# The experts' phase written out tile by tile, its value products shared between GpSimd and VectorE, attention blocks added in pairs, and weights loaded on condition

## The chip, the cores and the metric

The kernel runs on one core of one Trainium2 chip. The metric is the device time of one execution in microseconds; the time before is the median of three runs. The profile is of one further execution.

## The reference

All is float32. With x of [4, 2048, 256] the result is `x + attention(xn) + ffn(xn)`, where xn is x after a layer norm without gains.

`attention` works on each token alone, across its 16 heads of 16:

```python
Q, K, V = (xn @ Wq + bq), (xn @ Wk + bk), (xn @ Wv + bv)   # [b, s, 16, 16]
Q, K = rope(Q), rope(K)                    # one token's q and k turn by the same angles
score = einsum('bsid,bsjd->bsij', Q, K) / 4
out = einsum('bsij,bsjd->bsid', softmax(score), V)
```

`ffn` is a mixture block in two steps. The first, called `_mla`, projects queries, keys and values, computes a causal attention per head along 2048 positions and adds its output projection. The second, called `_moe`, takes the normed result row by row:

```python
logits = t @ gate_w                       # 8 experts
top_v, top_i = top_k(logits, 2)
gates = softmax(top_v)
hid = silu(t @ w1[e])                     # 256 -> 512
y   = hid @ w2[e]                         # 512 -> 256
out = sum over the row's two experts of gate * y
```

In the kernel, `attention` is done in blocks of 128 tokens, whose q, k and v stand in `head_qkv`: for each token 16 x 16 scores, their softmax and the product with v. Half of the 64 blocks are done earlier in the program, on GpSimd beside other work; the experts' phase does the other 32.

## The kernel before

The program has five phases: projections, attention along the positions, output projection and routing, experts, and the final store. The routing phase writes each token's row twice, once for each of its two experts, into `sorted_rows` (the profile's `rows_by_expert`), sorted by expert. It also makes `table_i`: for each of 71 tiles of 256 rows (`N_TILE`) the expert and the first row. Its first column is, for tile n, the number of experts whose tiles end at or before n (L1571 to L1580), so it never falls from one tile to the next. `acc` in DRAM collects the result.

`phase4_experts` does two things at once, on all engines.

The experts' part goes tile by tile. SP loads the tile's rows (`load_tile`, L1781, one of four buffers, `RB`; it waits until the add of tile n - 4 has landed, `y_added`), and the expert's two weight matrices, 512 KB each, into one of two buffers (L1784 and L1786; it waits until tile n - 2 is multiplied, `y_done`). PE transposes the rows (L1978), multiplies by w1 (L1990) and w2 (L2003); its order for a tile is `hidden(n)`, `transpose_rows(n + 1)`, `second(n)`. ScalarE applies SiLU (L1949), copies the transposed rows (L1923) and scales the result by the gate into `y` (L1966). GpSimd adds the tile into `acc` with two indirect scatters (`add_tile`, L1822). Before it issues them it waits until the add before has landed, that of the tile and that of the block, because both read and write rows of `acc`.

The blocks' part goes one block to two tiles. SP loads q, k and v of a block (`load_block`, L1772). ScalarE copies q to PSUM (L1929). VectorE multiplies q by k (L1870, 4096 elements a partition), sums over the head's 16 (L1873), takes the maximum (L1875) and subtracts it (L1879). ScalarE takes the exponential (L1936). VectorE sums the rows (L1884) and inverts (L1886). GpSimd multiplies the probabilities by v (`weigh_values`, L1806) in three pieces: 8 heads in the even tile, 4 and 4 in the odd one, with the block's own add (L1829, 128 KB from SBUF into 128 rows of `acc`) between the last two. VectorE sums these products (L1893) and multiplies by the inverse (L1896).

The order on each engine's queue is the order in which the code is written; nothing is scheduled at run time. The groups of four tiles (`quads`) run as a loop from the third group on, and so does VectorE's body. All waits are written by hand. Many are `wait_apart`, a wait with a second instruction that increments an unused semaphore.

## Time and profile before

| | |
|---|---|
| median of 3 runs | 3068.91 us (3065.43 to 3079.44) |
| the profiled execution, its own time | 3062.26 us |
| its span | 3060.5 us |
| PE busy | 2571.4 us, 84% |
| VectorE (DVE) busy | 2334.0 us, 76% |
| ScalarE (ACT) busy | 1572.3 us, 51% |
| GpSimd (POOL) busy | 2328.0 us, 76% |
| moved by DMA | 404.89 MB, mean 132 GB/s |
| weight transfers | 142 of 512 KB, each in one loop of two a tile |

The shares are means over the whole span; what bounds one phase is read from that phase. A row of the profile names the line of the kernel, the engine, the operation and the tiles, and the idle time before it with what ended it.

### The profile page before, as it was taken

The numbers are of one execution on the slowest core, as the hardware profiler recorded it, in microseconds if no ns is written. First come the engines' busy times: TensorE is split into PE (matmuls) and PEld (weight loads), VectorE is DVE, ScalarE is ACT, GpSimd is POOL, SyncE is SP. The second block draws the span as 40 slices with busy tenths as digits, with TensorE's granted clock in tenths as the row PEclk, the third lists the DMA queues.
The fourth block names the chain that finished last, engine by engine and source line by source line (L and its number), as shares of the span: only waits on it lengthen the run. The fifth ranks groups of instructions, "written<-read, shape, count | busy, mean of one in ns | idle before, by whom it ended". The sixth has DMA issues, their size and how long they took to land. (4 is left out here: it accounts for less than half of the span.)

```text
span 3060.5 us, 59749 instructions
## 1 busy us (share of the span) xinstructions
PE 2571.4 (84%) x21356; PEld 1316.2 (43%) x21356; DVE 2334.0 (76%) x3621; ACT 1572.3 (51%) x2325; POOL 2328.0 (76%) x1230
## 2 busy tenths in 40 slices
PE   7998978999999999999999999766757768777782
PEld 4544432333333333333333333255646656666662
DVE  4567858999999999998999984045639888988860
ACT  2322236777777767777677777622323333333330
POOL 5443359788988889888988889746748888888882
PEclk9999999999999999999999999877778989889886
DMA  5886541323332223332233311387566667666766
GB/s 195 273 269 203 180 149 52 85 51 86 82 88 77 64 84 82 90 79 64 82 83 85 75 40 42 97 259 252 171 186 171 164 167 167 170 163 164 173 160 165
DMA packets 296054, 404.89 MB, mean 132 GB/s; under 512 B 32040, under 2 KB 221832, under 8 KB 295560
## 3 DMA queue, kind: packets, MB, share of 16 engines
q1 hardware_dynamic: 264360, 357.80, 39.1%
q0 software_dynamic: 31200, 39.73, 7.6%
q10 hardware_dynamic: 256, 4.19, 0.4%
q8 instruction: 148, 2.42, 0.3%
q14 instruction: 90, 0.74, 0.1%
HBM read 251.16 MB, written 158.23 MB: 134 GB/s over the span
## 5 line engine op out<-in xcount | busy, mean ns | idle before, releaser
L1044 DVE TENSOR_REDUCE p_piece_max<-p_ring 128x1 f32<-128x512 f32 (+3 forms) x2160 | 1293.7, 654 | 137.4 <-PE p_ring L157 67.7
L1102 ACT ACTIVATE p_probs<-p_st 128x1024 f32<-128x1024 f32 (+3 forms) x1280 | 1079.0, 897 | 413.8 <-PE p_st L1165 216.6
L1165 PE MATMUL p_st<-unit_q,unit_k 64*128 64x512 bf16 (+3 forms) x3520 | 434.6, 349 | 42.1 <-ACT p_probs L1102 25.4
L1183 PE MATMUL p_pv<-p_probs,unit_vg 128*32 128x512 f32 (+3 forms) x3520 | 412.0, 542 | 0.0
L1806 POOL TENSOR_TENSOR p_pv<-p_pr,p_qkv 128x1024 f32<-128x1024 f32 (+1 forms) x96 | 403.1, 4206 | 1.4 <-ACT p_pr L1936 1.4
L982 POOL TENSOR_TENSOR p_terms<-p_head_p,p_head_in 128x4096 f32<-128x4096 f32 x32 | 348.5, 10890 | 0.1
L1822 POOL DMA_INDIRECT acc<-p_y,p_rows x142 | 224.8, 1583 | 105.2 <-issue 42.0
L2003 PE MATMUL p_y_ps<-p_w,p_hid 128*128 128x256 f32 x1136 | 300.4, 425 | 3.4 <-ACT p_hid L1949 3.3
L170 PE MATMUL p_ring<-unit_k,unit_q 64*128 64x512 bf16 (+3 forms) x1600 | 271.7, 353 | 27.9 <-DVE p_piece_max L1044 25.4
L961 POOL TENSOR_TENSOR p_terms<-p_head_in 128x4096 f32<-128x4096 f32 x32 | 283.4, 8856 | 8.2 <-POOL p_head_s L969 4.4
L1990 PE MATMUL p_hid_ps<-p_rT,p_w 128*128 128x256 f32 x1136 | 259.8, 382 | 7.1 <-issue 4.3
L988 POOL TENSOR_TENSOR p_terms<-p_terms 128x2048 f32<-128x2048 f32 (+2 forms) x96 | 252.4, 2630 | 17.1 <-POOL p_terms L988 11.4
L966 POOL TENSOR_TENSOR p_terms<-p_terms 128x2048 f32<-128x2048 f32 (+2 forms) x96 | 252.0, 2625 | 17.1 <-POOL p_terms L966 11.4
L2003 PEld LDWEIGHTS p_y_ps<-p_w,p_hid 128*128 128x128 f32 x1136 | 242.3, 219 | 43.9 <-issue 2.8
L1990 PEld LDWEIGHTS p_hid_ps<-p_rT,p_w 128*128 128x128 f32 x1136 | 216.4, 191 | 40.2 <-issue 10.7
L1165 PEld LDWEIGHTS p_st<-unit_q,unit_k 64*128 64x128 bf16 x3520 | 136.6, 95 | 219.9 <-ACT p_probs L1102 130.9
L170 PEld LDWEIGHTS p_ring<-unit_k,unit_q 64*128 64x128 bf16 x1600 | 71.4, 93 | 363.8 <-DVE p_piece_max L1044 351.1
L1978 PE MATMUL p_rT_ps<-ident,p_rows 128*128 128x128 f32 x284 | 54.6, 325 | 191.8 <-DMA p_rows<-rows_by_expert 191.8
L1893 DVE TENSOR_REDUCE p_oh<-p_pv 128x256 f32<-128x4096 f32 x32 | 141.4, 4420 | 96.1 <-POOL p_pv L1806 95.2
L1165 PE MATMUL p_st<-p_q,p_k 34*128 34x512 bf16 (+7 forms) x1600 | 194.3, 346 | 8.1 <-ACT p_probs L1102 6.7
L1183 PE MATMUL p_pv<-p_probs,p_vg 128*32 128x512 f32 (+3 forms) x1600 | 186.3, 540 | 0.0
L1445 POOL DMA_INDIRECT rows_by_expert<-p_th,p_pos x128 | 132.4, 1034 | 37.6 <-issue 34.8
(184 smaller groups left out, 3610.0 us busy)
## 6 DMA issues: line engine op xcount, KB each, us to landing
p_w<-ffn_w SPq DMA_DIRECT2D x142, 512.0 KB, 5.6
qk_parts<-p_parts SPq DMA_DIRECT2D x64, 384.0 KB, 3.4
head_qkv<-p_heads SPq DMA_DIRECT2D x16, 1536.0 KB, 6.5
p_rows<-rows_by_expert SPq DMA_DIRECT2D x71, 258.0 KB, 3.7
unit_q<-qk_parts SPq DMA_DIRECT2D x132, 128.0 KB, 3.2
unit_k<-qk_parts SPq DMA_DIRECT2D x132, 128.0 KB, 3.6
v_padded<-p_vx SPq DMA_DIRECT2D x16, 1024.0 KB, 8.2
p_head_in<-head_qkv SPq DMA_DIRECT2D x32, 384.0 KB, 4.0
```

Of the source, the lines that this page charges most:

```text
L170: last[half] = nc.tensor.matmul(banks[half][:, k * width:(k + 1) * width], q6[rows, h + k, i * P:(i + 1) * P], k6[rows, h + k, pc * CT:pc ...
L961: step(nc.gpsimd.tensor_tensor(terms[:, :, :, :], head_in[:, u, 0, :, :].unsqueeze(2).to_broadcast([P, H, H, DH]), head_in[:, u, 1, :, :]. ...
L966: step(nc.gpsimd.tensor_tensor(terms[:, :, :, 0:width], terms[:, :, :, 0:width], terms[:, :, :, width:2 * width], ALU.add), before + 2 + k)
L982: step(nc.gpsimd.tensor_tensor(terms[:, :, :, :], head_p[:, u, :, :].unsqueeze(2).to_broadcast([P, H, DH, H]), head_in[:, u, 2, :, :].rear ...
L988: step(nc.gpsimd.tensor_tensor(terms[:, :, :, 0:width], terms[:, :, :, 0:width], terms[:, :, :, width:2 * width], ALU.add), before + 2 + k)
L1044: nc.vector.tensor_reduce(piece_max[:, n % 2, h:h + heads, i, pc], ring_ps[g % RING][:, 0:heads * width].rearrange("p (h k) -> p h k", h=h ...
L1102: nc.scalar.activation(probs[:, 2 * turn_of(s, i) + u, :, 0:width], st_ps[u][:, :, 0:width], ACT.Exp).then_inc(probs_done, 1)
L1165: last = nc.tensor.matmul(st_ps[u][:, half, 0:width], k6[s][rows, PAIR * second + u, kt * P:(kt + 1) * P], q6[s][rows, PAIR * second + u, ...
L1183: last = nc.tensor.matmul(pv_ps[hh * VW:(hh + 1) * VW, skip:CT], vg[s][:, kt, hh * VW:(hh + 1) * VW], probs[:, 2 * turn_of(s, i) + hh % PA ...
L1806: ins = nc.gpsimd.tensor_tensor(pv[:, u, h, :, :], pr[:, u, h, :].unsqueeze(2).to_broadcast([P, count, DH, H]), qkv[:, u, 2, :].rearrange( ...
L1990: last = nc.tensor.matmul(hid_ps[i][:, f * ROW_TILE:(f + 1) * ROW_TILE], w1[:, u, k, (2 * i + f) * P:(2 * i + f + 1) * P], rT[:, k, :], st ...
L2003: last = nc.tensor.matmul(y_ps[t][:, 0:D], hid[:, f, t * P:(t + 1) * P], w2[:, u, f, :], start=f == 0, stop=f == FB - 1)
```

## The change

It touches `phase4_experts` alone.

- The loops over groups of four tiles are gone: each engine's code is written out for all 71 tiles and 32 blocks, with waits on constants and without the second instruction of `wait_apart`. Where a block's steps come among the tiles is in tables (`STARTS`, `WEIGHED`, `ADDED`, `STORED`, `LOADED`, `COPIED`, `SHIFTED`). With `SPAN` 64 and 32 blocks `STARTS[m]` is 2m, so a block still begins every two tiles.
- Of the 16 heads GpSimd multiplies ten (`HP`), five in each of two tiles. VectorE multiplies the other six in `weigh_tail`. ScalarE writes their probabilities to PSUM and the ten's to SBUF, with two exponentials.
- VectorE's sum of the products goes to PSUM (`o_ps`) instead of SBUF, and the multiplication by the inverse reads it there.
- Finished blocks are stored by SP into `attn_rows` in DRAM, and GpSimd adds two neighbouring blocks at once, 256 KB from DRAM, in the 16 tiles 10, 14, ..., 70; the tile's second piece of products is cut into three and two heads around it.
- q, k and v have three buffers (`QB`) instead of two. The first three blocks are loaded at tile 0, later ones a tile or two earlier than before.
- The two weight loads of a tile carry a condition: they are done only where the tile's expert is another than that of tile n - 2, whose weights lie in the same buffer.

The diff, cut to its core:

```diff
+
+    STARTS = [m * SPAN // NB for m in range(NB + 4)]
+    PIECES = {2: (5, 5), 3: (4, 3, 3)}
...
+    WEIGHED = {n: (m, heads, heads.stop == HP) for m in range(NB) for n, heads in pieces(m)}
+    ADDED = {STARTS[2 * k + 4] + 2: k for k in range(NB // 2)}
+    STORED = {STARTS[m + 2] + 3: m for m in range(NB)}
+    LOADED = {max(0, STARTS[m] - 1): m for m in range(QB, NB)}
+    COPIED = {STARTS[m]: m for m in range(NB)}
+    SHIFTED = {STARTS[m + 1]: m for m in range(NB)}
...
+            def load_block(m):
+                if m >= QB:
+                    sp.wait_ge(pv_done, m - QB + 1)
+                    sp.wait_ge(tail_done, m - QB + 1)
+                sp.dma_start(qkv[:, m % QB, :, :].rearrange("p i d -> p (i d)"), head_qkv[block_of(m, 1)]
+                             ).then_inc(qkv_loaded[m % QB], 16)
+
+            def store_block(m):
+                sp.wait_ge(oh_done, m + 1)
+                sp.dma_start(attn_rows[block_of(m, 1)], oh[:, m % 2, :, :].rearrange("p i d -> p (i d)")
+                             ).then_inc(oh_stored[m % 2], 16)
+
+            experts = []
+            for n in range(N_TILE):
+                u = n % 2
+                e = sp.value_load(table_i[0:1, 0, n:n + 1], min_val=0, max_val=E - 1)
+                row = sp.value_load(table_i[0:1, 1, n:n + 1], min_val=0, max_val=SORTED - ROW_TILE)
+                if n >= RB:
+                    sp.wait_ge(y_added, 16 * RT * (n - RB + 1))
+                sp.dma_start(rows[:, n % RB, :, :], sorted_rows[bass.ds(row, ROW_TILE), :].rearrange("(t p) d -> p t d", p=P)
+                             ).then_inc(rows_loaded[n % RB], 16)
+                if n >= 2:
+                    sp.wait_ge(y_done, n - 1)
+                changed = None if n < 2 else e != experts[n - 2]
+                sp.dma_start(w1[:, u, :, :], w["ffn_w1"][bass.ds(e, 1), :, :].rearrange("a (k p) f -> p (a k) f", p=P),
+                             cond=changed).then_inc(w_loaded[u], 16)
+                sp.dma_start(w2[:, u, :, :], w["ffn_w2"][bass.ds(e, 1), :, :].rearrange("a (k p) f -> p (a k) f", p=P),
+                             cond=changed).then_inc(w_loaded[u], 16)
+                experts.append(e)
+                if n == 0:
+                    for m in range(QB):
+                        load_block(m)
+                if n in LOADED:
+                    load_block(LOADED[n])
+                if n in STORED:
+                    store_block(STORED[n])
...
+            def weigh(m, heads, last):
+                pool.wait_ge(exp_done, m + 1)
+                if m >= 2:
+                    pool.wait_ge(o_done, m - 1)
+                u, count = m % 2, heads.stop - heads.start
...
+            pairs = [0]
+
+            def add_tile(n):
+                pool.wait_ge(y_copied, n + 1)
+                if n:
+                    pool.wait_ge(y_added, 16 * RT * n)
+                if pairs[0]:
+                    pool.wait_ge(pair_added, 16 * pairs[0])
...
+            def add_pair(k, tiles):
+                for u in range(2):
+                    pool.wait_ge(oh_stored[u], 16 * (k + 1))
+                pool.wait_ge(y_added, 16 * RT * tiles)
+                n = block_of(2 * k, 1)
+                rows_of_pair = lambda a: a.rearrange("(r s) d -> r (s d)", s=8)
+                nc.gpsimd.dma_start(rows_of_pair(acc[n * P:(n + 2) * P, :]),
+                                    rows_of_pair(attn_rows[n:n + 2, :, :].rearrange("a p d -> (a p) d")),
+                                    accum_op=ALU.add, max_dma_last_dim=4 * 8 * D).then_inc(pair_added, 16)
+                pairs[0] += 1
+
+            for n in range(N_TILE):
+                if n:
+                    add_tile(n - 1)
+                weighed = WEIGHED.get(n)
+                if n not in ADDED:
+                    if weighed:
+                        weigh(*weighed)
+                    continue
+                if weighed:
+                    m, heads, last = weighed
+                    weigh(m, slice(heads.start, heads.stop - 2), False)
+                add_pair(ADDED[n], n)
+                if weighed:
+                    weigh(m, slice(heads.stop - 2, heads.stop), last)
+            add_tile(N_TILE - 1)
+            pool.wait_ge(y_added, 16 * RT * N_TILE)
+            pool.wait_ge(pair_added, 16 * NB // 2)
...
+            def weigh_tail(m):
+
+                u, count = m % 2, H - HP
+                dve.wait_ge(exp_done, m + 1)
+                nc.vector.tensor_reduce(psum[:, 0:HP], pr[:, u, :, :], AX_X, ALU.add)
+                nc.vector.tensor_reduce(psum[:, HP:], s_ps[u][:, HP:, :], AX_X, ALU.add).then_inc(psum_done, 1)
+                nc.vector.tensor_tensor(
+                    pv[:, u, HP:, :, :],
+                    s_ps[u][:, HP:, :].unsqueeze(2).to_broadcast([P, count, DH, H]),
+                    qkv[:, m % QB, 2, :].rearrange("p (j d) -> p d j", d=DH).unsqueeze(1).to_broadcast([P, count, DH, H]),
+                    ALU.mult).then_inc(tail_done, 1)
+                dve.wait_ge(psum_done, m + 1)
                 nc.vector.reciprocal(inv[:, u, :], psum[:, :]).then_inc(inv_done, 1)
...
+            def finish(m):
+                u = m % 2
+                dve.wait_ge(pv_done, m + 1)
+                dve.wait_ge(tail_done, m + 1)
+                nc.vector.tensor_reduce(o_ps[:, u * D:(u + 1) * D].rearrange("p (i d) -> p i d", d=DH), pv[:, u, :, :, :],
+                                        AX_X, ALU.add).then_inc(o_done, 1)
+                dve.wait_ge(o_done, m + 1)
+                dve.wait_ge(inv_done, m + 1)
+                if m >= 2:
+                    dve.wait_ge(oh_stored[u], 16 * (m // 2))
+                nc.vector.tensor_tensor(oh[:, u, :, :], o_ps[:, u * D:(u + 1) * D].rearrange("p (i d) -> p i d", d=DH),
                                         inv[:, u, :].unsqueeze(2).to_broadcast([P, H, DH]), ALU.mult).then_inc(oh_done, 1)
...
+            for m in range(NB + 2):
+                if m >= 2:
+                    finish(m - 2)
+                if 0 < m <= NB:
+                    weigh_tail(m - 1)
+                if m < NB:
+                    score(m)
...
+            def probabilities(m):
+                u = m % 2
+                act.wait_ge(sm_done, m + 1)
+                if m >= 2:
+                    act.wait_ge(inv_done, m - 1)
+                    act.wait_ge(pv_done, m - 1)
+                nc.scalar.activation(pr[:, u, :, :], sm[:, 0:HP, :], ACT.Exp)
+                nc.scalar.activation(s_ps[u][:, HP:, :], sm[:, HP:, :], ACT.Exp).then_inc(exp_done, 1)
```

## Rows read from the trace of the kernel before

**Rows 1.** The page's first line: the span.

```profile
span 3060.5 us, 59749 instructions
```

**Rows 2.** Windows, 2300 to 2957 us: window, length, busy time (instructions), clock, DMA, GB/s.

```profile
2300.00:2957.00 657.00, 497.42 (x2160) 420.33 (x2159) 575.60 (x239) 248.24 (x419) 548.22 (x238) 0.89 0.69 167
```

**Rows 3.** Groups by form, same window: busy us, mean ns | idle before, releasers.

```profile
L1806 POOL TENSOR_TENSOR p_pv<-p_pr,p_qkv 128x1024 f32<-128x1024 f32 x60 | 197.4, 3291 | 0.0
L1822 POOL DMA_INDIRECT acc<-p_y,p_rows x118 | 187.1, 1586 | 49.1 <-issue 37.9 <-DMA acc<-p_y,p_rows 7.5 <-DMA acc<-p_oh 3.7
...
L1806 POOL TENSOR_TENSOR p_pv<-p_pr,p_qkv 128x2048 f32<-128x2048 f32 x30 | 181.3, 6045 | 0.0
L1896 DVE TENSOR_TENSOR p_oh<-p_oh,p_inv 128x256 f32<-128x256 f32 x30 | 145.9, 4863 | 2.3
...
L1893 DVE TENSOR_REDUCE p_oh<-p_pv 128x256 f32<-128x4096 f32 x29 | 128.2, 4420 | 72.0 <-POOL p_pv L1806 71.1 <-DMA acc<-p_oh 0.6 <-issue 0.3
...
L1829 POOL DMA_DIRECT2D acc<-p_oh x30 | 27.7, 923 | 59.6 <-DMA acc<-p_y,p_rows 54.1 <-ACT p_pr L1936 3.9 <-issue 1.5
...
L1879 DVE TENSOR_TENSOR p_sm<-p_q_ps,p_smax 128x256 f32<-128x256 f32 x30 | 12.7, 424 | 1.0
...
L1884 DVE TENSOR_REDUCE p_psum<-p_pr 128x16 f32<-128x256 f32 x30 | 12.2, 406 | 0.0
...
L1886 DVE RECIPROCAL p_inv<-p_psum 128x16 f32<-128x16 f32 x30 | 7.6, 253 | 1.0
```

**Rows 4.** Lines L1896 and L1870 by themselves: duration min/median/max, first and last start.

```profile
L1896 DVE TENSOR_TENSOR p_oh<-p_oh,p_inv x32: 424/4746/5844, 2297.5 to 2983.4; 128x256 f32<-128x256 f32 x32
...
L1870 DVE TENSOR_TENSOR p_prod<-p_q_ps,p_qkv x30: 4359/4361/4364, 2302.9 to 2944.3; 128x4096 f32<-128x4096 f32 x30
```

**Rows 5.** The chain that ended last: start us, us, what.

```profile
2646.82 6.85 DMA acc<-p_y,p_rows
...
2656.45 6.12 DMA acc<-p_y,p_rows
...
2982.80 3.70 DMA acc<-p_y,p_rows
...
2989.23 6.05 DMA acc<-p_y,p_rows
```

**Rows 6.** DMA issues, median us to landing; then landing times of L1829, of L1822.

```profile
p_w<-ffn_w SPq DMA_DIRECT2D x122, 512.0 KB, 5.7
p_rows<-rows_by_expert SPq DMA_DIRECT2D x61, 258.0 KB, 3.7
...
DMA to landing us min/median/max: 2.8/3.1/5.4
...
DMA to landing us min/median/max: 3.7/5.1/7.7
```

**Rows 7.** Timeline, VectorE near 2288, GpSimd near 2970 and 3022 us.

```profile
2287.84 0.42 DVE L1879 TENSOR_TENSOR p_sm<-p_q_ps,p_smax 128x256 f32<-128x256 f32 x1
...
2970.54 1.55 POOL L1822 DMA_INDIRECT acc<-p_y,p_rows  x1 [0.30 <-issue]
2971.55 3.37 POOL L1806 TENSOR_TENSOR p_pv<-p_pr,p_qkv 128x1024 f32<-128x1024 f32 x1
2974.94 0.93 POOL L1829 DMA_DIRECT2D acc<-p_oh  x1
...
3022.59 1.56 POOL L1822 DMA_INDIRECT acc<-p_y,p_rows  x1 [0.30 <-issue]
```

**Rows 8.** Timeline of SP's queue, two stretches.

```profile
2643.67 0.35 SPq L1772 DMA_DIRECT2D p_qkv<-head_qkv  x1
...
2646.81 0.42 SPq L1786 DMA_DIRECT2D p_w<-ffn_w  x1
...
2975.67 0.98 SPq L1786 DMA_DIRECT2D p_w<-ffn_w  x1
...
2987.35 0.37 SPq L1784 DMA_DIRECT2D p_w<-ffn_w  x1
```

More of the change, by code:

```diff
@@ L1691, in phase4_experts, with pieces @@
     sorted_rows, acc, table_i = SHARED["sorted"], SHARED["acc"], SHARED["table"]
-    QUADS, ALL_QUADS = NB // 2, (N_TILE + 3) // 4
-    IN_LAST = N_TILE - 4 * (ALL_QUADS - 1)
     RT = ROW_TILE // P
     FB = F // P
-    RB = 4
+    RB, QB = 4, 3
+    HP = 10
+    SPAN = 64
+    STARTS = [m * SPAN // NB for m in range(NB + 4)]
+    PIECES = {2: (5, 5), 3: (4, 3, 3)}
+    def pieces(m):
+        tiles = range(STARTS[m + 1], STARTS[m + 2])
+        counts = PIECES[len(tiles)]
+        return [(n, slice(sum(counts[:k]), sum(counts[:k + 1]))) for k, n in enumerate(tiles)]
+    WEIGHED = {n: (m, heads, heads.stop == HP) for m in range(NB) for n, heads in pieces(m)}
[4 more added lines that the diff above has]
+    SHIFTED = {STARTS[m + 1]: m for m in range(NB)}
+    assert all(ADDED[n] * 2 + 1 in [m for at, m in STORED.items() if at < n] for n in ADDED)
+    assert max(ADDED) < N_TILE and max(STORED) < N_TILE and len(ADDED) == NB // 2 and len(LOADED) == NB - QB
     with ExitStack() as ctx:
@@ L1732, in phase4_experts @@
         y_added = sem("p4_y_added")
-        qkv_loaded = [sem(f"p4_qkv_loaded{i}") for i in range(2)]
+        qkv_loaded = [sem(f"p4_qkv_loaded{i}") for i in range(QB)]
         q_copied = sem("p4_q_copied")
@@ new lines, in _ @@
+            copy_rows(0)
+            for n in range(N_TILE):
+                for k in range(2):
+                    act.wait_ge(hid_done, 2 * n + k + 1)
+                    if n:
+                        act.wait_ge(y_done, n)
+                    nc.scalar.activation(hid[:, 2 * k:2 * k + 2, :].rearrange("p k t -> p (k t)"), hid_ps[k][:, :],
+                                         ACT.Silu).then_inc(silu_done, 1)
+                if n + 1 < N_TILE:
+                    copy_rows(n + 1)
+                if n in SHIFTED:
+                    probabilities(SHIFTED[n])
+                if n in COPIED:
+                    copy_q(COPIED[n])
+                act.wait_ge(y_done, n + 1)
+                if n >= RB:
+                    act.wait_ge(y_added, 16 * RT * (n - RB + 1))
+                for t in range(RT):
+                    last_copy = nc.scalar.activation(y[:, n % RB, t, :], y_ps[t][:, 0:D], ACT.Copy,
+                                                     scale=rows[:, n % RB, t, D:D + 1])
+                last_copy.then_inc(y_copied, 1)
@@ L1993, in hidden, with second @@
                     last.then_inc(hid_done, 1)
-            def second(n, u):
-                pe.wait_ge(y_copied, n)
+            def second(n):
+                if n:
+                    pe.wait_ge(y_copied, n)
                 for k in range(2):
-                    pe.wait_ge(silu_done, 2 + 2 * n + k + 1)
+                    pe.wait_ge(silu_done, 2 * n + k + 1)
                     for t in range(RT):
                         for f in range(k * FB // 2, (k + 1) * FB // 2):
-                            last = nc.tensor.matmul(y_ps[t][:, 0:D], hid[:, f, t * P:(t + 1) * P], w2[:, u, f, :],
+                            last = nc.tensor.matmul(y_ps[t][:, 0:D], hid[:, f, t * P:(t + 1) * P], w2[:, n % 2, f, :],
                                                     start=f == 0, stop=f == FB - 1)
                 last.then_inc(y_done, 1)
-            transpose_rows(0, 0, 1)
-            def body(g):
-                for i in range(tiles_of(g)):
-                    n, u = 4 * g + i, i % 2
-                    hidden(n, u, 2 * g + i // 2)
-                    if not (static(n) and n == N_TILE - 1):
-                        transpose_rows(n + 1, (i + 1) % RB, g + 1 + (i + 1) // RB)
-                    second(n, u)
-            quads(pe, body)
+            transpose_rows(0)
+            for n in range(N_TILE):
+                hidden(n)
+                if n + 1 < N_TILE:
+                    transpose_rows(n + 1)
+                second(n)
 def phase5_combine(nc, apart, res_v, attn_v, pos_v, gates_v, expert_rows, out_v):
```

208 lines of the change are left out of this document (38 added, 170 removed).

## The prediction

> **What bounds the kernel now.** I read the page first, for the span [rows 1]. Shares of the whole span decide nothing here, since the change touches only the experts' phase (lines 1685 to 2017), so I cut that stage out. Its block 1 is scored at 2287.84 us and its last scatter is issued at 3022.59 us [rows 7]. In the even middle of it PE is busy 76%, VectorE 88%, GpSimd 83% and the DMA engines 69% [rows 2]. Again nobody is full, so something is waited for in turn. VectorE's product (L1870) starts at 2302.9 for the first and at 2944.3 for the last of 30 blocks [rows 4]: 641.4 / 29 = 22.1 us a block, which is two tiles, 11.06 us a tile.
>
> The chain that ended last says what those 22.1 us are [rows 5]. It is the adds into acc, one after the other: a tile's second scatter starts at 2646.82 and takes 6.85 us to land, the next tile's starts at 2656.45 and takes 6.12, then the block's own add. The step from a landing to the next tile's second scatter is 2656.45 - 2646.82 - 6.85 = 2.8 us (1.9 from one scatter to the next, as their 1.59 and 0.3 of issue make it, so some 0.9 from a landing until GpSimd starts again). So: 2.8 + 6.5 for a tile, the same for the next, and for the block's add 3.1 in the median [rows 6] with 0.9 to pick it up: 22.6, against 22.1 measured. GpSimd's products lie in the shadows of these landings: its waits for landings sum to only 54.1 + 7.5 + 3.7 us [rows 3], so it is the second bound, close behind. VectorE waits 72 us for GpSimd's products before L1893. PE waits for rows that are loaded late, a consequence.
>
> Two facts decide the rest. First, why a landing takes 6.5 us. The one from 2982.80 takes 3.70; the last weight load before it was issued at 2975.67, seven us earlier. The one from 2989.23 takes 6.05, with a weight load issued at 2987.35 and the next one right behind [rows 5, 8]. While GpSimd multiplies it can be short too: the scatter at 2970.54 had landed when the block's add, which waits for it, began at 2974.94, so in under 4.4 us, though a product ran from 2971.55 [rows 7]. So it is the weights in flight, not GpSimd's work. Second, L1896, 256 elements, takes 4746 ns in the median and 424 at least [rows 4]. L1879 has as many elements and takes 424 in the mean [rows 3]; it has one operand in PSUM, L1896 both in SBUF, and L1896's longest, 5844, stays just under GpSimd's product of 6045. It is held while GpSimd multiplies, not slow.
>
> **The change, part by part.**
> - Weights. The table of experts does not fall along the tiles (L1571 to L1580 count the experts that lie behind), so there are at most 7 changes, and each reloads at most both buffers: 2 + 14 = 16 tiles load instead of 71, 32 transfers instead of 142. That takes 110 / 71 x 0.5 MB, some 0.8 MB, of each tile's traffic away. The landing should fall to 3.7 to 4.4 us on most tiles; I take 4.0. The rest of the traffic (rows, 258 KB in 3.7 us [rows 6]) stays beside it.
> - GpSimd's products. Ten heads instead of 16, in two pieces of five. From 1024 elements in 3.29 and 2048 in 6.05 us [rows 3], 2.69 ns an element: 1280 take 3.98. A tile's two scatters take 2 x 1.59 + 0.3, less 0.56 where the product's row overlaps: 2.9. With 0.17 of hand-over a plain tile is 7.05 us of GpSimd. The landing chain of the same tile is 2.8 + 4.0 = 6.8. These are level, so GpSimd sets it.
> - The pair's add: 16 of 256 KB from DRAM instead of 32 of 128 KB from SBUF, each in one tile of four. The trace has no such transfer. Bounds: 2.8 us below (fastest block's add) and 7.7 above (the slowest landing of any scatter) [rows 6]; I take 4.5, nearer to the block's add, since its bytes double and its issue is the same instruction. That tile: 1.9 + 4.0 + 0.9 until the pair is issued (three heads, 2.6 us, lie inside), then 4.5 + 0.9 until the next scatter (two heads inside): 12.2. Four tiles: 3 x 7.05 + 12.2 = 33.3, or 16.7 a block.
> - VectorE. Removed: L1896's hold, 4.86 down to 0.42, because its input moves to PSUM. Added: the product of six heads, 1536 elements; L1870 gives 4096 in 4.36 and L1879 256 in 0.42, so 1.03 ns an element and 1.74 us; the row sums in two parts, 0.31 + 0.24 instead of 0.41. A block is 4.36 + 4.42 (L1873, a sum of 4096 like L1893's) + 0.42 (the maximum, of 256 like L1884's 0.41) + 0.42 (scores), 4.42 + 0.42 (finish), 1.74 + 0.55 + 0.25 (tail): 17.0, and with some 0.03 in each of ten joints 17.3 us [rows 3, 4]. That is above GpSimd's 16.7, so **VectorE becomes the bound**.
> - Does anything feed VectorE late? After its maximum is subtracted (time s), ScalarE's exponential is done at s + 1.0; GpSimd has the two pieces by s + 12 in a plain round and s + 16.3 in one with a pair. VectorE wants them at s + 17.3. The slack is 1 us in each second round, used up when the pair's landing reaches 5.5. ScalarE waits for s in order, with the y copies behind it and PE's second product behind those. Until it is back at that place it has at most its own work of a block and half of PE's before it. Its own is 248.2 us over 29.7 blocks, 8.4; PE's is 2160 matmuls at 36 a tile, so 60 tiles in 497.4, 8.3 each at a mean clock of 0.89, 7.4 at full clock, 14.8 a block [rows 2]. 8.4 + 7.4 = 15.8 is inside 17.3, and so is PE by itself.
> - SP. load_block still waits for GpSimd, but three blocks deep and one block earlier; the rows behind it come at s + 17.5 to 21.5, wanted by 21.4. store_block waits for work finished by then. I count nothing for it; VectorE covers it, and without that cover it is some 1 us in each second round. The second instruction of each wait goes away and the loops are written out, also under VectorE's cover, where at most the 0.6 us a tile that stands as "issue" before scatters (37.9 us over 59 tiles [rows 3]) could be gained without it.
>
> Some of these near misses will cost; I add 0.4 to the floor of 17.3 and take **17.7 us a block**.
>
> **The sum.** Block 1 is scored at 2287.84 now [rows 7], by the pace of the tiles, and block 2 can't come before; with the tail product it is 2291. Block 31: 2291 + 30 x 17.7 = 2822. Then seven tiles remain: block 31's products until s + 12, pair 14 until s + 25, four tiles at 2.8 + 3.7 = 6.5, pair 15, the last scatter: s + 58.5. Last scatter at 2880.5; behind it the same 3060.5 - 3022.59 = 37.9: span 2918.4, 142 us less than 3060.5. The execution's own time lies 1.8 above its span, 3062.3, and the median of the runs 6.6 above that: 3068.9 - 142 = **2927**.
>
> **A rule weighed.** The row: the block's add, 128 KB, lands in 3.1 us in the median [rows 6]. The Trainium skill (DMA: Bandwidth & Descriptors, Anatomy of one DMA) fits a GpSimd-issued transfer as 2.0 us plus the bytes at 436 GB/s, 2.3 us for this one. The trace here is 0.8 above. By the rule the pair would land in 2.6 and GpSimd's four tiles be 31.4; the sum, set by VectorE, would be the same.
>
> **The rivals.**
> - *The feeding is late.* Pair landing of 7.7, or the shared order of ScalarE and SP, makes GpSimd 36.5 a four, 18.3, and the joints cost another 0.7: 19.0 a block, 2966. For it: 1 us of slack. Against: the weights loading beside the scatters, which made the longest landings, are mostly gone. 0.22.
> - *The landing stays at 6.5*, because rows and GpSimd's own traffic suffice, or because the condition does not skip. Then a tile is 9.2, the pair's 14.6: 42.2 a four, 21.1 a block; 2291 + 633, about 100 more than my case: 3029. Against: 3.70 at 2982.80 [rows 5]. 0.08.
> - *The tail product is held like L1896.* GpSimd starts its product at the same exponential, 4.0 long: 21.3 a block, 3035. Against: L1870, one operand in PSUM, takes 4359 to 4364 in all 30 with GpSimd busy 83% [rows 2, 4]. The Trainium skill (SBUF — State Buffer, SBUF: two separate sides) has VectorE and GpSimd exclude each other only for two SBUF inputs or a two-port mode; by that the tail is free, at 17.3. 0.04.
> - *Slower: conditional transfers are dear on SP.* Its queue needs now some 3.6 us from one block load (2643.67) through the rows' load to the end of the tile's second weight load (2646.81 + 0.42) [rows 8]. It decides above 11.2 us a tile (22.4 a block brings back the old time), so (11.2 - 3.6) / 2 = 3.8 for each of two transfers. If a skipped one held the queue as long as a real one takes to land, 5.7 [rows 6], a tile is 15.0 and a block 30.0: 30 x 12.3 = 369 more than my case, 3296. The lower end is a skip that costs no more than an issue now, 0.42, and that is hidden. No row shows a condition; I lean to the low end, since nothing in a skip has to wait for data. 0.04.
>
> **Chances and range.** My case 0.62 (2895 to 2950 alone). Faster by over 0.5% 0.94, same 0.02, slower 0.04; the before runs spread 0.46%, so about 0.5% is what can be told. Below: no waits at all, 17.0 a block (-21), and a tail at PE's pace (-10), 2896. Above: 19.9 a block, +66, 2993. Range 2895 to 2990 leaves out the last three rivals, 0.16.
>
> **What the profile would show.** L1896's successor at 0.42; the tail product at 1.7; VectorE at 95% or more of the middle stage, with its wait for GpSimd near nothing; scatters that land in 4 us; 32 weight transfers at the most; PE's clock near full, since its pauses for rows shrink. I am wrong if landings stay above 5.5, if the pair's takes over 6, or if VectorE waits above 1 us a block.

## The result and the profile after

| | before | after |
|---|---|---|
| median of 4 runs | 3071.62 us (3065.43 to 3079.44) | 2926.18 us (2925.28 to 2926.78) |
| ratio | | 0.9519, 95% interval 0.9500 to 0.9538 |
| span of the profiled execution | 3060.5 us | 2923.9 us |

The kernel is 145 us faster. The predicted 2927 us and the measured time agree within 1 us, but not all terms do. First the page of the kernel after: the span, the busy times, and SP's DMA queue.

```profile
span 2923.9 us, 58265 instructions
...
PE 2546.4 (87%) x21356; PEld 1302.0 (45%) x21356; DVE 2283.6 (78%) x3685; ACT 1570.9 (54%) x2357; POOL 2180.7 (75%) x1196
...
q1 hardware_dynamic: 224968, 304.32, 35.1%
```

The same row of the kernel before:

```profile
q1 hardware_dynamic: 264360, 357.80, 39.1%
```

SP's queue moved 357.80 MB before. It now carries 4.19 MB of block stores more, so 357.80 + 4.19 - 304.32 = 57.7 MB are gone: at 0.524 MB each, 110 transfers. 32 of 142 were done: SP's queue shows them in tiles 0, 1, 8, 9, 16, 17, 25, 26, 34, 35, 41, 42, 50, 51, 58 and 59, two each.

The window in the middle of the experts' phase, as in [rows 2]:

```profile
2300.00:2800.00 500.00, 444.36 (x2046) 382.15 (x2044) 495.15 (x282) 236.69 (x430) 390.57 (x196) 0.95 0.60 126
```

VectorE was 88% busy and is 99%. GpSimd fell from 83 to 78%. PE's granted clock rose from 0.89 to 0.95, while its wait for rows before the transposes fell from 154.8 us in 657 to 41.9 in 480; that the one made the other is not shown.

Groups by form, 2320 to 2800 us of the kernel after, against [rows 3]:

```profile
L1835 POOL DMA_INDIRECT acc<-p_y,p_rows x108 | 170.1, 1575 | 77.2 <-issue 36.1 <-DMA acc<-attn_rows 24.9 <-ACT p_y L1963 14.8
L1818 POOL TENSOR_TENSOR p_pv<-p_pr,p_qkv 128x1280 f32<-128x1280 f32 x42 | 169.7, 4041 | 4.6 <-ACT p_q_ps L1943 4.6
...
L1905 DVE TENSOR_REDUCE p_o_ps<-p_pv 128x256 f32<-128x4096 f32 x28 | 123.7, 4418 | 1.0 <-POOL p_pv L1818 1.0
...
L1893 DVE TENSOR_TENSOR p_pv<-p_q_ps,p_qkv 128x1536 f32<-128x1536 f32 x27 | 74.4, 2757 | 0.0
...
L1845 POOL DMA_DIRECT2D acc<-attn_rows x13 | 11.5, 884 | 7.4 <-DMA acc<-p_y,p_rows 5.2 <-DVE p_o_ps L1905 1.6 <-issue 0.5
```

VectorE's sum L1905 (L1893 before) waited 71.1 us for GpSimd's products in 657 us; now it waits 1.0 in 480. GpSimd has idle time instead, most of it before its scatters: 24.9 us for the pair's add to land and 14.8 for `y`. The tail product, L1893 now, takes 2757 ns where I had 1740.

Lines by themselves: duration min/median/max in ns, first and last start; then landing times of the tiles' scatters (L1835) and of the pairs' adds (L1845).

```profile
L1911 DVE TENSOR_TENSOR p_oh<-p_o_ps,p_inv x32: 423/424/427, 2304.6 to 2848.2; 128x256 f32<-128x256 f32 x32
...
DMA to landing us min/median/max: 3.6/4.0/7.5
...
DMA to landing us min/median/max: 4.0/4.6/5.5
```

L1911 is L1896's successor: 4746 ns in the median before [rows 4], 424 each time now. One block of VectorE in the timeline (start us, us):

```profile
2600.67 0.42 DVE L1884 TENSOR_TENSOR p_sm<-p_q_ps,p_smax 128x256 f32<-128x256 f32 x1
2601.01 4.42 DVE L1905 TENSOR_REDUCE p_o_ps<-p_pv 128x256 f32<-128x4096 f32 x1
2605.46 0.42 DVE L1911 TENSOR_TENSOR p_oh<-p_o_ps,p_inv 128x256 f32<-128x256 f32 x1
2605.80 0.31 DVE L1891 TENSOR_REDUCE p_psum<-p_pr 128x10 f32<-128x160 f32 x1
2606.03 0.25 DVE L1892 TENSOR_REDUCE p_psum<-p_q_ps 128x6 f32<-128x96 f32 x1
2606.20 2.76 DVE L1893 TENSOR_TENSOR p_pv<-p_q_ps,p_qkv 128x1536 f32<-128x1536 f32 x1
2608.88 0.24 DVE L1899 RECIPROCAL p_inv<-p_psum 128x16 f32<-128x16 f32 x1
2609.04 4.35 DVE L1875 TENSOR_TENSOR p_prod<-p_q_ps,p_qkv 128x4096 f32<-128x4096 f32 x1
2613.43 4.43 DVE L1878 TENSOR_REDUCE p_q_ps<-p_prod 128x256 f32<-128x4096 f32 x1
2617.89 0.42 DVE L1880 TENSOR_REDUCE p_smax<-p_q_ps 128x16 f32<-128x256 f32 x1
2618.35 0.42 DVE L1884 TENSOR_TENSOR p_sm<-p_q_ps,p_smax 128x256 f32<-128x256 f32 x1
```

From one L1884 to the next is 17.68 us, with no idle stretch. The ten durations sum to 18.02: where a row does not need the one before, it starts 0.08 us before that one's end (2601.01 against 2600.67 + 0.42), so the joints give time back.

SP's queue nearby: a tile's two weight loads skipped, the next tile's rows load, and the first of that tile's weight loads, done.

```profile
2602.05 0.09 SPq L1798 DMA_DIRECT2D p_w<-ffn_w  x1
2602.24 0.08 SPq L1800 DMA_DIRECT2D p_w<-ffn_w  x1
2604.22 0.39 SPq L1793 DMA_DIRECT2D p_rows<-rows_by_expert  x1
2609.74 0.39 SPq L1798 DMA_DIRECT2D p_w<-ffn_w  x1
```

A skipped one holds the queue for 0.08 to 0.09 us here, a done one for 0.39.

Where the 136.6 us of span came from, by the starts of the subtraction: from block 1 to block 31 it took 2953.65 - 2287.84 = 665.8 us and takes 2831.38 - 2299.79 = 531.6, 134.2 less. The tiles after block 31 take 56.3 instead of 68.9 (12.6 less) and what follows 36.2 instead of 37.9 (1.7 less). Against this block 1 starts 12.0 us later, of which 9.8 lie ahead of the phase: its first weight load is issued at 2255.5 us instead of 2245.7.

### The profile page after: what moved, and what is told of

It is laid out like the page before. It is cut to its first block and busy times, and to the rows that moved or that the text cites. A ratio compares the mean times of both kernels' runs of the same rounds, so it can differ in the third digit from the quotient of the medians.

```text
span 2923.9 us, 58265 instructions
## 1 busy us (share of the span) xinstructions
PE 2546.4 (87%) x21356; PEld 1302.0 (45%) x21356; DVE 2283.6 (78%) x3685; ACT 1570.9 (54%) x2357; POOL 2180.7 (75%) x1196
## 3 DMA queue, kind: packets, MB, share of 16 engines
q1 hardware_dynamic: 224968, 304.32, 35.1%
q10 hardware_dynamic: 256, 4.19, 0.4%
## 5 line engine op out<-in xcount | busy, mean ns | idle before, releaser
L1165 PE MATMUL p_st<-unit_q,unit_k 64*128 64x512 bf16 (+3 forms) x3520 | 433.1, 348 | 41.6 <-ACT p_probs L1102 24.9
L1835 POOL DMA_INDIRECT acc<-p_y,p_rows x142 | 223.4, 1573 | 135.8 <-ACT p_y L1963 49.5
L2000 PE MATMUL p_y_ps<-p_w,p_hid 128*128 128x256 f32 x1136 | 278.9, 402 | 11.1 <-ACT p_hid L1951 10.8
L1818 POOL TENSOR_TENSOR p_pv<-p_pr,p_qkv 128x1280 f32<-128x1280 f32 (+2 forms) x78 | 259.6, 3328 | 26.8 <-ACT p_q_ps L1943 26.8
L2000 PEld LDWEIGHTS p_y_ps<-p_w,p_hid 128*128 128x128 f32 x1136 | 226.0, 204 | 45.2 <-issue 13.2
L1875 DVE TENSOR_TENSOR p_prod<-p_q_ps,p_qkv 128x4096 f32<-128x4096 f32 x32 | 139.6, 4364 | 30.0 <-ACT p_q_ps L1934 30.0
L1905 DVE TENSOR_REDUCE p_o_ps<-p_pv 128x256 f32<-128x4096 f32 x32 | 141.4, 4418 | 4.9 <-POOL p_pv L1818 4.9
```

The costliest lines, as they stand in the source:

```text
L1165: last = nc.tensor.matmul(st_ps[u][:, half, 0:width], k6[s][rows, PAIR * second + u, kt * P:(kt + 1) * P], q6[s][rows, PAIR * second + u, ...
L1818: ins = nc.gpsimd.tensor_tensor(pv[:, u, heads, :, :], pr[:, u, heads, :].unsqueeze(2).to_broadcast([P, count, DH, H]), qkv[:, m % QB, 2, ...
L2000: last = nc.tensor.matmul(y_ps[t][:, 0:D], hid[:, f, t * P:(t + 1) * P], w2[:, n % 2, f, :], start=f == 0, stop=f == FB - 1)
```

## The experiments

All kernels below compute the whole reference. "Period" is the mean distance of the blocks' subtractions, from block 1 to block 31, in the profiled execution: 22.19 us before, 17.72 after. A round is the time from one block's subtraction to the next one's; a plain round has no pair's add on GpSimd. Kernels that ran beside one another are compared by medians, others also by their ratio to the kernel before.

### Each part undone

**All weights loaded.** In the kernel after:

```diff
-                changed = None if n < 2 else e != experts[n - 2]
+                changed = None
```

> The changed kernel with the condition taken off the weight loads: both are done for each of the 71 tiles. My theory: weights in flight lengthen the landings of the scatters (4.5 us in the median with the condition, 5.1 before), the chain of adds becomes the bound again, 42.2 us for four tiles or 21.1 a block instead of 17.7: 30 x 3.4 = 102 us more, about 3028. Rival, the gain is VectorE's and GpSimd's shorter work alone and the landings stay hidden behind products: 17.7 a block, 2926, within 0.5%. A middle result of 18.5 to 20 a block (2950 to 2995) would say that the landings lengthen, but less than the earlier chain had it.

Measured: 2976.28 us (2961.18 to 3003.86), ratio 0.9648 (0.9607 to 0.9688). That is 40 (by ratios) to 50 us (by medians) given back, half of what I expected. (The 4.5 us in the expectation is a slip: with the condition the scatters land in 4.0.) The profiled execution was its slowest: its span is 78 us above that of the kernel after. Its group of VectorE's sum, 2320 to 2800 us, and the landings of L1835 and L1845:

```profile
L1905 DVE TENSOR_REDUCE p_o_ps<-p_pv 128x256 f32<-128x4096 f32 x25 | 110.5, 4422 | 45.2 <-POOL p_pv L1818 45.1
...
DMA to landing us min/median/max: 3.6/4.9/8.4
...
DMA to landing us min/median/max: 4.1/6.1/7.6
```

The landings rise by 0.9 and 1.5 us with the weights in flight, and the wait for GpSimd is back. But rounds without a pair's add still take 17.7 to 17.9 us; those with one, but for the first, take 18.5 to 26.6. So a plain round has cover for a longer landing, and only the pair's tile lets it through.

Why less than the 102 us: the first six rounds stay at 17.7. Beyond that, the chain waits for the second scatter of a tile, the last to land in all 71, and how long that one takes depends on when the weights come. In the kernel before, 53 of the 71 second scatters had a weight load issued between 0.5 us ahead of them and 2 us behind, as here (a piece of the chain, then SP's queue):

```profile
2613.20 6.21 DMA acc<-p_y,p_rows
...
2613.80 0.37 SPq L1784 DMA_DIRECT2D p_w<-ffn_w  x1
```

These 53 landed in 6.7 us in the median, and the six with no weight load near them (none from 6 us ahead until they landed) in 3.8. In the new order with all weights 32 of 71 meet a load in that way and land in 6.7 too; over all 71 the median is 5.1, where it was 6.4 in the kernel before. I had carried the 6.5 of the old order into the new one. How much of the shortfall this makes, and why the runs spread from 2961 to 3004 us, is not shown.

**Value sum back in SBUF.** L1905 sums into `oh`, L1911 reads it there:

```diff
-                nc.vector.tensor_reduce(o_ps[:, u * D:(u + 1) * D]..., pv[:, u, :, :, :],
+                nc.vector.tensor_reduce(oh[:, u, :, :], pv[:, u, :, :, :],
...
-                nc.vector.tensor_tensor(oh[:, u, :, :], o_ps[:, u * D:(u + 1) * D]...,
+                nc.vector.tensor_tensor(oh[:, u, :, :], oh[:, u, :, :],
```

The wait for the earlier store of `oh` moves ahead of the sum with it.

> The changed kernel with the sum of the value products back in SBUF, so that the multiplication by the inverse has both operands in SBUF. My theory: it is held while GpSimd multiplies; GpSimd's piece now lies differently, from about s + 1.9 to s + 5.9 where VectorE wants to multiply at s + 4.8, so a hold of 0 to 1.5 us in a plain round and up to 3 in others: the row L1911 has a least value of 424 ns and a mean of 1.2 to 2.5 us, a block takes 18.4 to 19.8, the time is 2947 to 2990. Rival: the hold in the kernel before was a waiting for something else, and the row stays at 424: 2926.

Measured: 2936.43 us (2935.57 to 2940.65), ratio 0.9537 (0.9505 to 0.9569), period 18.18. The multiplication by itself:

```profile
L1910 DVE TENSOR_TENSOR p_oh<-p_oh,p_inv x32: 424/1038/2449, 2303.1 to 2860.0; 128x256 f32<-128x256 f32 x32
```

It is held again, up to 2449 ns, but takes 1.0 us in the median and not 4.7, and 0.9 in the mean, where I expected 1.2 to 2.5. The block and the time also stay below what I expected. GpSimd's product lies differently beside it in this order of work. With two SBUF inputs it is held, with one in PSUM it never was (427 at most). The Trainium skill (SBUF — State Buffer, SBUF: two separate sides) has just this condition, and both traces agree. The move to PSUM is worth 10 us by the medians and 5 by the ratios in this order of work, not the 4.3 us a block that the old order would suggest.

**Blocks added one by one**, each in its own tile, still from DRAM:

```diff
-    ADDED = {STARTS[2 * k + 4] + 2: k for k in range(NB // 2)}
+    ADDED = {STARTS[m + 4]: m for m in range(NB)}
```

> The changed kernel with each block added alone, 128 KB from DRAM, in every second tile, instead of two at once in every fourth. My theory: GpSimd's four tiles hold two waits for landings instead of one: 2 x 7.05 + 2 x (1.9 + 4.0 + 0.9 + 3.7 + 0.9 = 11.4) = 36.9, 18.5 a block against VectorE's 17.7, so 20 to 30 us more, about 2950. Rival, VectorE covers it since GpSimd has slack in plain rounds: same time, 2926.

Measured: 2973.66 us (2970.22 to 2979.08), ratio 0.9655 (0.9621 to 0.9689), period 18.93: 42 to 48 us given back, about twice what I expected. Its sum L1904, the adds' group with their waits, 2320 to 2800 us, and their landing:

```profile
L1904 DVE TENSOR_REDUCE p_o_ps<-p_pv 128x256 f32<-128x4096 f32 x26 | 115.1, 4425 | 30.7 <-POOL p_pv L1818 30.7
...
L1844 POOL DMA_DIRECT2D acc<-attn_rows x24 | 20.8, 868 | 42.2 <-DMA acc<-p_y,p_rows 42.2
...
DMA to landing us min/median/max: 3.3/3.6/4.3
```

Two blocks cost 2 x 3.6 of landing apart and 4.6 together, but what weighs as much is the wait before each add: 42.2 us for the scatter ahead of it, against 5.2 with pairs.

**All 16 heads on GpSimd**, in two pieces of eight:

```diff
-    HP = 10
+    HP = 16
...
-    PIECES = {2: (5, 5), 3: (4, 3, 3)}
+    PIECES = {2: (8, 8), 3: (6, 5, 5)}
```

> The changed kernel with all 16 heads' value products on GpSimd, eight in each of two tiles, none on VectorE. My theory: GpSimd takes 6.05 + 2.9 + 0.17 = 9.1 us in a plain tile and 13.1 in one with a pair, 40.5 for four, 20.2 a block, and VectorE's 15 lie inside: 30 x 2.5 = 76 us more, about 3002. Rival, the products lie in the shadow of the landings as they did before (chain of a tile 2.8 + 4.0 = 6.8, under 9.1 only if landings stay short), and the share given to VectorE brought nothing: 2926.

Measured: 3004.97 us (3003.21 to 3010.86), ratio 0.9755 (0.9724 to 0.9787), period 19.96, for the most part rounds of 18.3 and 21.8 in turn. In 2320 to 2800 us VectorE's sum, L1897, waits as the row says:

```profile
L1897 DVE TENSOR_REDUCE p_o_ps<-p_pv 128x256 f32<-128x4096 f32 x24 | 106.3, 4428 | 117.1 <-POOL p_pv L1817 117.1
```

So the sharing is the dearest single part, 73 to 79 us, and GpSimd bounds without it, as reckoned.

### Parts done alone on the kernel before

**The condition only**, in `load_tile`:

```diff
+                changed = e != sp.value_load(table_i[0:1, 0, bass.ds(n - 2, 1)], min_val=0, max_val=E - 1)
...
-                             ).then_inc(w1_loaded[u], 16)
+                             cond=changed).then_inc(w1_loaded[u], 16)
```

> The kernel before with one part of the change alone: the condition on the weight loads (with one more register load a tile on SP). My theory: its chain of landings shortens. The even tile is then set by GpSimd's own 9.1 us, the odd tile by 1.9 + 4.3 + 0.9 for the scatter and 3.1 + 0.9 for the block's add, 11.1: 20.2 a block instead of 22.1, 60 us less, a ratio of 0.98. Rival 1, weights in flight do not matter by themselves: ratio 1.00. Rival 2, all of the landing's surplus was the weights' and the products are hidden entirely: 18.0 a block, a ratio of 0.96.

Measured: 3006.10 us (3002.97 to 3007.78), ratio 0.9750 (0.9734 to 0.9766), period 20.19 where 20.2 was expected. The multiplication that was L1896, then the landings of the scatters and of the blocks' adds:

```profile
L1899 DVE TENSOR_TENSOR p_oh<-p_oh,p_inv x32: 424/4754/5340, 2308.0 to 2928.5; 128x256 f32<-128x256 f32 x32
...
DMA to landing us min/median/max: 3.6/3.9/8.1
...
DMA to landing us min/median/max: 3.0/3.1/4.0
```

This is the cleanest evidence for the first step: nothing but the weights changed (and one register load a tile), the scatters' landing went from 5.1 [rows 6] to 3.9, that of the second scatters alone from 6.4 to 3.9, and GpSimd's wait for landings before a block's add from 54.1 us in 657 to 5.2 in 480. The two profiled executions lie 59 us apart, as expected, the medians 77. What is left is the held multiplication, still 4754 ns: VectorE is 96% busy, with 4.3 us a block of it hold, and GpSimd 93%.

**Written out only**: the loops and second instructions gone and three buffers for q, k and v, with every other part undone (all weights, 16 heads on GpSimd, the sum in SBUF, single adds from SBUF in the old tiles).

```diff
-    ADDED = {STARTS[2 * k + 4] + 2: k for k in range(NB // 2)}
+    ADDED = {STARTS[m + 2] + 1: m for m in range(NB)}
```

> All parts of the change undone except the writing out (and three buffers for q, k and v): all weights loaded, 16 heads on GpSimd in 8, 4 and 4, the sum in SBUF, each block added alone from SBUF after the odd tile's scatters. My theory: the loops and the second instruction of each wait lay beside the chain of landings; at most 0.6 us a tile of issue, mostly hidden: a ratio of 0.990 to 1.00. Rival: writing out by itself brings 2% or more, by earlier loads and no loop ends, 0.98 or less.

Measured: 3098.30 us (3092.19 to 3104.38), ratio 1.0077 (1.0048 to 1.0106), period 23.08. Written out alone brings nothing and costs 0.8% (0.5 to 1.1), a little above the range that I expected. The landing of its scatters is 5.3 us in the median and that of the second ones 6.8 (6.4 before), with the chain of adds as the bound as before: two a block make some 0.7 of the 0.9 us. Why they land later was not isolated.

### What the tail product costs, and what is behind it

**Values turned for VectorE.** L1893 reads v with a step of 16 elements. ScalarE writes a copy in the order that VectorE reads (0.64 us), and only VectorE uses it:

```diff
+                nc.scalar.copy(vt[:, m % 2, :, :], qkv[:, m % QB, 2, :].rearrange("p (j d) -> p d j", d=DH)).then_inc(vt_copied, 1)
...
-                    qkv[:, m % QB, 2, :].rearrange("p (j d) -> p d j", d=DH).unsqueeze(1).to_broadcast([P, count, DH, H]),
+                    vt[:, u, :, :].unsqueeze(1).to_broadcast([P, count, DH, H]),
```

> The changed kernel where ScalarE copies the block's values, turned so that the 16 that are multiplied together lie side by side, and VectorE's tail product reads this copy. One more wait and one copy of 256 elements a block on ScalarE, GpSimd as before. My theory: the tail product takes 2.76 us instead of 1.74 because it reads its values with a step of 16 elements, so it falls to some 1.7 us, a block to 16.7, and with GpSimd's own 16.7 to 17 behind it the time falls by 20 to 30 us, about 2900. Rival: it is the operand in PSUM with a short repeat, or GpSimd at work on the same tiles; then the row stays at 2.76 and the time at 2926.

Measured: 2923.32 us (2915.94 to 2926.27), ratio 0.9473 (0.9453 to 0.9494), period 17.59. VectorE's sum in 2320 to 2800 us, and the tail product, L1896 here:

```profile
L1908 DVE TENSOR_REDUCE p_o_ps<-p_pv 128x256 f32<-128x4096 f32 x28 | 123.8, 4423 | 26.5 <-POOL p_pv L1820 26.5
...
L1896 DVE TENSOR_TENSOR p_pv<-p_q_ps,p_vt 128x1536 f32<-128x1536 f32 x28 | 48.9, 1747 | 0.0
```

The product falls from 2757 to 1747 ns, so the step was the whole of my error in it. The time hardly moves by the medians (3 us) and by the profiled spans (2923.9 and 2922.9). By the ratios it is 14 us, but the kernel before varied by 12 us from one series to the next and the kernel after by 1, so I go by the medians. Plain rounds take 16.67 us and are 1.0 shorter. Rounds with a pair take 17.0 to 18.2 and 19.8 to 21.0 in turn from block 11 on, since VectorE now waits 26.5 us for GpSimd, and GpSimd for its own adds:

```profile
L1837 POOL DMA_INDIRECT acc<-p_y,p_rows x108 | 170.1, 1575 | 82.4 <-issue 42.0 <-DMA acc<-attn_rows 33.6 <-ACT p_y L1969 6.6
```

The long ones come behind the tiles that still load weights. From one pair's add to the next, GpSimd's four tiles take 33.3 to 35.3 us where no weights are loaded meanwhile, and 34.8 to 38.7, four of five above 36, where those of two tiles are; VectorE's floor for them is 33.3. Scatters issued near these loads land in 5.4 us in the median, all others in 3.9. That the weights cause the delay is shown by the condition alone above; here it is the timing that speaks for it. GpSimd's floor is right behind VectorE's.

**Eleven heads on GpSimd**, to test that from the other side (`HP = 11`, pieces of six and five; v as in the kernel after):

> The changed kernel with 11 heads on GpSimd (six and five) and five on VectorE. My theory, VectorE is the bound and GpSimd has slack: VectorE's block loses 0.46 and is 17.2, GpSimd's four tiles gain 2 x 0.69 and are 34.7, 17.3 a block: 10 to 14 us less, about 2914. Rival, GpSimd and its landings are level with VectorE already: 18.0 a block or more, 2930 to 2945.

Measured: 2932.82 us (2929.89 to 2933.89), ratio 0.9509 (0.9493 to 0.9524), period 17.73. The time is in the rival's range, but the period is neither the 17.3 of my theory nor the rival's 18.0: plain rounds take 17.24 us as expected, but from block 13 on most rounds with a pair take 18.35 and more, so that the mean is that of the kernel after. What VectorE gains GpSimd takes back.

**Values turned and nine heads** (`HP = 9`, pieces of five and four):

> The kernel of values_turned with nine heads on GpSimd (five and four) and seven on VectorE. If the turned copy makes a head cost VectorE 0.27 us instead of 0.46, VectorE's block is 16.9 and GpSimd's 16.2: VectorE alone is the bound, about 2903, equal to or 5 us above values_turned. If values_turned is held by GpSimd's 16.7 to 17.2, this is the faster one, down to 2895. If turning brings nothing, a block is 18.1 and the time 2940.

Measured: 2913.99 us (2909.56 to 2917.60), ratio 0.9450 (0.9431 to 0.9468), period 17.20, plain rounds 16.93. This is 9 us less than with ten heads and turned values, run beside it, though VectorE's plain round is 0.26 longer: GpSimd did hold that kernel. It does not reach 2903, since late rounds are left, of 18.4 to 19.1 us, the first at block 17. The tail product of seven heads takes 2015 ns, so a turned head costs VectorE the 0.27 us that I took.

**Values turned, uneven pieces.** Ten heads, but eight and two in the rounds with a pair's add. The add lies in the first of the round's two tiles, within the block's first piece of five heads (not the second), which it cuts into three and two. Here that piece has eight heads, cut into four and four:

```diff
-        counts = PIECES[len(tiles)]
+        counts = (8, 2) if m % 2 == 0 and m >= 4 else PIECES[len(tiles)]
...
-                    weigh(m, slice(heads.stop - 2, heads.stop), last)
+                    weigh(m, slice(heads.stop - 4, heads.stop), last)
```

> The kernel of values_turned (ten heads on GpSimd), where in the rounds with a pair's add GpSimd multiplies eight heads in the pair's tile, four before and four after its issue, and only two in the next tile. Theory: the surplus of values_turned over VectorE's 16.67 (17.59 in the mean, in the rounds with a pair) is GpSimd's lateness; the two waits for landings in the pair's tile, 4.3 and 4.9 us, hold four heads each for nothing, so GpSimd gains 2 us in each such round and VectorE's 16.7 holds in nearly all: 27 us less than values_turned, a ratio of 0.940 to 0.943. Rival: the joints are SP's and ScalarE's order, and the pieces' place changes nothing: 0.947.

Measured: 2912.28 us (2911.46 to 2914.34), ratio 0.9471 (0.9444 to 0.9498), period 17.24. That is 11 us below the even pieces by the medians of two series, and nothing by the ratios, which give just the rival's 0.947. The periods (17.59 and 17.24) and the profiled spans (2922.9 and 2910.5) side with the medians, but the two never ran beside one another, so the gain of the pieces alone is not settled, and it is less than half of the 27 us that I expected. The kernel after, again beside it:

> The changed kernel as it is, beside the others on one chip, to have their differences without that of the chips. Ratio 0.950 to 0.954, a block 17.7, no theory differs.

Measured: 2924.97 us (2924.71 to 2932.29), ratio 0.9518 (0.9489 to 0.9546). Turning and uneven pieces together bring 12.7 us against it.

**Values turned for both engines**, with the uneven pieces: the turned copy has three buffers, and GpSimd's product reads it too.

```diff
-                    qkv[:, m % QB, 2, :].rearrange("p (j d) -> p d j", d=DH).unsqueeze(1).to_broadcast([P, count, DH, H]),
+                    vt[:, m % QB, :, :].unsqueeze(1).to_broadcast([P, count, DH, H]),
```

> The kernel of turned_split where GpSimd too reads the turned copy (three buffers of it). If the step of 16 elements costs GpSimd as it costs VectorE, its 1280 elements fall from 4.05 us to some 2.6 and a block is set by VectorE alone, 16.67, a ratio of 0.939. If GpSimd does not mind the step, its rows stay at 2.7 ns an element and the time is that of turned_split.

Measured: 2903.17 us (2900.38 to 2905.45), ratio 0.9438 (0.9406 to 0.9470), period 16.99, most rounds 16.67. It is 21.8 us below the kernel after beside it, and 9.1 below the one with uneven pieces alone. GpSimd's products, first with uneven pieces only, then with this edit:

```profile
L1820 POOL TENSOR_TENSOR p_pv<-p_pr,p_qkv 128x1280 f32<-128x1280 f32 x29 | 118.2, 4076 | 2.1 <-ACT p_q_ps L1949 2.1
L1820 POOL TENSOR_TENSOR p_pv<-p_pr,p_qkv 128x1024 f32<-128x1024 f32 x26 | 83.0, 3194 | 4.3 <-ACT p_q_ps L1949 4.3
```

```profile
L1820 POOL TENSOR_TENSOR p_pv<-p_pr,p_vt 128x1280 f32<-128x1280 f32 x30 | 102.5, 3415 | 5.1 <-ACT p_q_ps L1950 5.1
L1820 POOL TENSOR_TENSOR p_pv<-p_pr,p_vt 128x1024 f32<-128x1024 f32 x28 | 74.7, 2667 | 12.2 <-ACT p_q_ps L1950 12.2
```

The step costs GpSimd too: 0.66 us in 1280 elements and 0.53 in 1024, less than half of what I allowed for (4.05 to 2.6). The ratio stays above 0.939: five rounds of 17.9 to 19.8 us are left. GpSimd's four tiles take 31.2 to 33.9 us while at most one tile's weights are loaded, and 36.3 to 37.4 with those of two.

## Why the prediction was right, and where its terms were not

- **What bounded the kernel before**: shown. With the condition alone the landings shorten and the block falls by 2.0 us. The 6.5 us a landing, from two steps of the chain, was right as well: the chain waits for a tile's second scatter, which is the last to land and does so in 6.4 us in the median of 71, and the 5.1 of [rows 6] mixes it with the first, 4.3. Two tiles make 2 x (2.8 + 6.4) + 4.0 = 22.4, against 22.2 measured. [rows 3] also bounded what shorter landings alone could bring: GpSimd waited 54.1 + 7.5 + 3.7 us in 29.7 blocks, 2.2 a block.
- **110 transfers skipped, landing 4.0**: 110, and 4.0 in the median. But it is no even 4.0: the 14 tiles that load weights within the phase still have long ones (5.4 near such loads), and the prediction priced every landing alike.
- **L1896's hold**: gone in all 32 blocks, and back when its inputs are both in SBUF.
- **VectorE becomes the bound, 17.7 a block**: 99% busy, 17.72. But that the sum meets the measured block so closely is luck: errors cancel. The tail product was priced at 1.74 us by L1870, whose inputs are read in order; with the step it is 2.76, 1.02 too little. On the other side I gave 0.03 for each of ten joints. The four where a row needs the one before it cost 0.03 to 0.04, but the other six overlap by 0.08, and together they give back 0.34 (18.02 of durations, 17.68 of period), 0.64 too much; and of the 0.4 for near misses only 0.04 was used (17.72 against 17.68). 1.02 - 0.64 - 0.36 = 0.02.
- **GpSimd's 16.7 a block**: near where no weights are loaded, too low in the mean. Its product was right (4.04 against 3.98) and so was the pair's landing (4.6 against 4.5). With VectorE's floor at 16.67 (values turned) four tiles without weight loads take 33.3 to 35.3 us, where I had 33.3, but over tiles 10 to 58, with the loads, the mean is 35.8, or 17.9 a block. So by this timing the term that was too small is, for the most part, the landing of scatters beside the remaining weights. The longer tail product, which put VectorE at 17.7, covered it.
- **Feeding late** (0.22): not in this kernel, 1.0 us of wait in 28 blocks. It is what the turned kernels ran into: GpSimd late in rounds with a pair. **Landing stays at 6.5**: no. **Tail product held**: no, 2812 ns at the longest in any of 32.
- **Conditional transfers dear**: no. A skip takes 0.10 us of SP's queue at most and 0.07 in the median, below even the lower end that I gave it.
- **The end terms**: block 1 at 2299.8 instead of 2291. Most of this is not the change: the profiled execution of before reached the phase early, with its first weight load at 2245.7 us, and the 13 other traces have it at 2254.8 to 2263.0, also the one with the old loops and the condition alone (2256.5, block 1 at 2298.4). From that load to block 1 it takes 44.3 us instead of 42.1, where I had 3.2 more. The tail was 56.3 us (58.5 predicted) and the rest 36.2 (37.9). 2299.8 + 531.6 + 56.3 + 36.2 = 2923.9 of span; 2918.4 was predicted, 5.5 too little. The median makes up for it by luck: I put it 6.6 above the profiled execution, as before, and it is 0.5 above.
- **The rule weighed**: the Trainium skill's fit (DMA: Bandwidth & Descriptors, Anatomy of one DMA) gives 2.6 us for the pair's add. The trace disagrees, 4.0 at the least and 4.6 in the median. Two terms of mine are 0.1 off among the rivals (2.8 + 6.5 is 9.3, not 9.2, and the pair's tile with it 14.7); neither changes a chance.
- **Parts do not add**: undone one at a time they give back 50, 10, 48 and 79 us, 187 together, for a change of 145; the condition alone brought 77 on the kernel before. Undoing any one brings back a bound, whatever the others have removed. The writing out was not undone on the kernel after; alone it brings nothing.

## What to carry to other kernels

Price a new instruction by a row that reads its operands in the same order, not only by one of equal size; v was read with a step in GpSimd's product all along, which was the hint. No row of the kernel before had VectorE read in that way, so the term had no price of its own, and the range has to allow for that. When two engines come out level, a sum that names one as the bound says little about what the next microsecond off that engine will bring: look at both floors, then give the other one work away in the same edit, as the last kernel does. A transfer that nobody waits for can still be the bound, by making those that are waited for land later. A median over two kinds of instruction (a tile's first and second scatter) can hide the one that the chain waits for.

## What the runs showed of the hardware

- A float32 operand in SBUF read with a step of 16 elements: VectorE, with its other operand in PSUM, takes 2757 ns instead of 1747 for 1536 elements (58% more), GpSimd 4076 instead of 3415 for 1280 (19% more). The Trainium skill (SBUF — State Buffer, Door 1: The DMA port swizzle) tells of 16-byte lines in SBUF and of a penalty where each access goes to a new one; the trace agrees in direction, and the page gives no size. By that rule the tail product would have been dearer than L1870's slope, which the prediction missed.
- An accumulating transfer of GpSimd lands in 3.1 us with 128 KB from SBUF, 3.6 with 128 KB from DRAM, 4.6 with 256 KB from DRAM, and 6.1 with 256 KB when all weights are loaded beside it (medians).
- The same scatters land in 3.9 to 4.2 us in the median in the kernels that skip weights and in 4.9 to 5.3 in those that load all. Second scatters with a weight load issued within 0.5 us ahead to 2 us behind them: 6.7 us; with none near: 3.8.
- A skipped transfer keeps SP's queue for 0.07 us in the median and 0.10 at most in the kernel after, a done one for about 0.4.
- VectorE's multiplication with two inputs in SBUF took 424 ns at the least and 4746 in the median beside GpSimd's products; with one input in PSUM 427 at the most.
- VectorE's instructions that do not depend on one another start 0.08 us before the one ahead has ended; those that do start 0.03 to 0.04 after it.
